# State space scan of the first block: input product made by GpSimd, decays in PSUM, sum over the states by adding DMAs

## What is computed

```
xc = silu(conv(x_proj));  dt = softplus(...);  A = -exp(A_log)
dA  = exp(dt * A[:, n])              # decay
dBx = (dt * xc) * B[:, n]            # u * B, the scan's input
h_t = dA_t * h_(t-1) + dBx_t         # along the 64 tokens of a sequence
y   = sum over n of h * C[:, n]
y   = (y + D * xc) * silu(z);  out = y @ out_proj.T
```

## Time and profile before

| | us |
|---|---|
| median of three executions | 2637.21 |
| the profiled execution | 2636.14 |
| its span | 2634.3 |

### The profile page before, as it was taken

The page is one execution under the profiler, slowest core; times in us unless marked ns, Lnnn a source line. Parts: engine busy times, 40 slices in busy tenths (PEclk is TensorE's granted clock), DMA queues, the critical chain, the costliest instruction groups (busy, mean ns, idle before and its releaser), DMA issues.

```text
span 2634.3 us, 24845 instructions
## 1 busy us (share of the span) xinstructions
PE 2179.9 (83%) x7195; PEld 1194.3 (45%) x7200; DVE 1954.9 (74%) x1963; ACT 1148.6 (44%) x2464; POOL 388.9 (15%) x310
## 2 busy tenths in 40 slices
PE   6765667988888869988898869988888869699997
PEld 2222223434554434434454434434444434588883
DVE  3699995469999986269999986269999984454543
ACT  2623330465555532265565531266565530344441
POOL 0000000001111111001111111001111111556640
PEclk9778778889999989989999989989999989799999
DMA  1210120126777761226777762226777662321210
GB/s 56 81 32 24 32 84 24 65 94 146 167 155 151 162 160 54 89 93 141 161 152 161 155 145 75 89 84 138 160 153 164 155 142 79 104 78 62 80 52 16
DMA packets 89533, 277.38 MB, mean 105 GB/s; under 512 B 10208, under 2 KB 10336, under 8 KB 87424
## 3 DMA queue, kind: packets, MB, share of 16 engines
q1 hardware_dynamic: 61056, 173.85, 21.2%
q0 software_dynamic: 28416, 102.77, 21.0%
HBM read 167.27 MB, written 4.46 MB: 65 GB/s over the span
## 4 chain that ended last, share of the span: by engine, by line
DVE 36%; PE 32%; issue 17%; ACT 10%; DMA 2%; DVEq 1%; ACTq 0%; POOL 0%; SPq 0%; POOLq 0%
DVE hs L947 13%; DVE hs L938 6%; PE acc L1218 4%; DVE hs L954 4%; PE pq L1263 3%; ACT dA L737 3%; PE acc L1342 3%; PE pq L1488 3%; PE pk L1488 2%; DMA xc<-hs 2%; DVE qp L960 2%; DVE qr L964 2%; PE pq L1271 2%; ACT qr L681 2%; ACT qr L680 2%
## 5 line engine op out<-in xcount | busy, mean ns | idle before, releaser
L947 DVE TENSOR_TENSOR_SCAN hs<-dA,hs 128x1024 f32<-128x1024 f32 x256 | 572.9, 2285 | 0.0
L737 ACT ACTIVATE dA<-dt,aneg 128x504 f32<-128x504 f32 x512 | 337.3, 709 | 511.0 <-DVE hs L947 501.8
L603 POOL DMA_DIRECT2D xc<-hs x192 | 166.3, 876 | 1443.8 <-DVE hs L954 1356.2
L1271 PE MATMUL pq<-qT,wa 128*128 128x512 f32 x768 | 347.7, 607 | 34.4 <-DVE sc L995 34.4
L1353 PE MATMUL acc<-wb,oT 128*128 128x512 f32 x768 | 365.2, 622 | 3.5 <-ACT oT L726 3.5
L938 DVE TENSOR_TENSOR hs<-u,bc 128x1024 f32<-128x1024 f32 x256 | 302.3, 1227 | 7.8 <-ACT xc L823 7.8
L954 DVE TENSOR_TENSOR hs<-hs,bc 128x1024 f32<-128x1024 f32 x256 | 305.6, 1210 | 0.0
L707 ACT ACTIVATE pr<-sc,mx 128x64 f32<-128x64 f32 x512 | 170.8, 335 | 193.1 <-DVE mx L1001 193.1
L1271 PEld LDWEIGHTS pq<-qT,wa 128*128 128x128 f32 x768 | 145.7, 194 | 213.6 <-issue 187.4
L1218 PE MATMUL acc<-xnT,wa 128*128 128x512 f32 x512 | 229.2, 601 | 11.9 <-PE acc L1218 4.4
L1353 PEld LDWEIGHTS acc<-wb,oT 128*128 128x128 f32 x768 | 146.4, 200 | 156.5 <-issue 151.8
(11 more groups left out here) (191 smaller groups left out, 3038.1 us busy)
## 6 DMA issues: line engine op xcount, KB each, us to landing
xc<-hs POOLq DMA_DIRECT2D x192, 512.0 KB, 5.7
bc<-bc_rows SPq DMA_DIRECT2D x64, 512.0 KB, 7.5
wa<-in_wq SPq DMA_DIRECT2D x64, 512.0 KB, 10.1
wb<-in_wo SPq DMA_DIRECT2D x64, 512.0 KB, 3.3
wa<-in_wx SPq DMA_DIRECT2D x16, 512.0 KB, 3.6
wa<-in_wz SPq DMA_DIRECT2D x16, 512.0 KB, 3.5
wb<-in_ow SPq DMA_DIRECT2D x16, 512.0 KB, 4.7
wk<-in_wk SPq DMA_DIRECT2D x32, 256.0 KB, 10.2
```

The costliest lines, as they stand in the source:

```text
L603: G.dma_start(xc[:, 2 * c:2 * c + 2, :], hs[:, c, :].rearrange("p (d t) -> p d t", t=T), accum_op=ALU.add).then_inc(s_y[c], 16)
L737: ins = S.activation(to[:, :, 1:SEQ], dt[:, s, :].rearrange("p (b t) -> p b t", t=SEQ)[:, :, 1:SEQ], ACT.Exp, scale=aneg[:, s, bass.ds(jj ...
L947: V.tensor_tensor_scan(out=hs[:, c, :], data0=dA[:, c % 2, :], data1=hs[:, c, :], initial=0.0, op0=ALU.mult, op1=ALU.add).then_inc(scd.sem, 1)
L1271: ins = M.matmul(pq[:, h, :], wa4(p)[:, k, h * P:(h + 1) * P], qT[:, k, :], start=(k == 0), stop=(k == KE - 1))
```

## The change

It is confined to stage 0 (`mamba and not attn`).

- GpSimd makes the scan's input u * B (`feed`), into a ring of two buffers of its own, `qp` and `qr`, which belong to the attention and are free in stage 0. Ahead of the product of chunk k it issues the adding DMA of chunk k-3 (`begin_sum`), which first waits for the product with C of k-3; the product itself waits for the scan of k-2.
- ScalarE writes the decays into PSUM (`pq` for even chunks, `pk` for odd ones). VectorE clears the first token of each sequence there, once.
- VectorE's chunk step (`scan_alone`, `state_alone`) is scan(k) from PSUM and the ring into `hs`, then the product with C of chunk k-1. A scan waits for the adding DMA of chunk k-4, which still reads the same `hs[:, c]`.
- TensorE's zero matmuls and `sum_y` are gone, and so are VectorE's additions of the banks (L1100). The sum goes into `xc` by 64 adding DMAs.

```
+        def decays(c):
+            return (pq if c % 2 == 0 else pk)[:, :, :].rearrange("p d t -> p (d t)")
+        inputs = [x[:, :, :].rearrange("p a t -> p (a t)") for x in (qp, qr)]
...
 gpsimd:
+                def begin_sum(k, at):
+                    c = k % NCH
+                    eng.wait_ge(hcd.sem, hcd.upto(0, k) + at)
+                    hold(eng)
+                    G.dma_start(xc[:, 2 * c:2 * c + 2, :], hs[:, c, :].rearrange("p (d t) -> p d t", t=T),
+                                accum_op=ALU.add).then_inc(s_y[c], 16)
+                def feed(jj, p, c, first):
+                    k, at = NCH * p + c, jj * (2 * NCH)
+                    if not first or c == 3:
+                        begin_sum(k - 3, at)
+                    if c == 0:
+                        eng.wait_ge(s_bc[p], jj * 16 + 16)
+                        hold(eng)
+                    eng.wait_ge(scd.sem, scd.upto(0, k - 2) + at)
+                    hold(eng)
+                    G.tensor_tensor(
+                        inputs[c % 2].rearrange("p (d t) -> p d t", t=T), u[:, 2 * c:2 * c + 2, :],
+                        bc[:, p, 0:1, :].to_broadcast([P, 2, T]), ALU.mult).then_inc(inr.sem, 1)
+                if mamba and not attn:
+                    eng.wait_ge(y0r.sem, y0r.upto(0, NCH - 1))
+                    for p in range(2):
+                        for c in range(NCH):
+                            feed(0, p, c, p == 0)
+                    with eng.Fori(1, NS // 2) as jj:
+                        for p in range(2):
+                            for c in range(NCH):
+                                feed(jj, p, c, False)
+                    for k in range(NS * NCH - 3, NS * NCH):
+                        begin_sum(k, 0)
+                    for c in range(NCH):
+                        eng.wait_ge(s_y[c], 16 * NS)
+                    eng.sem_inc(yad.sem, NS * NCH)
...
 scalar (decay, and ahead of the first one):
-                        to = dA[:, c % 2, d * T:(d + 1) * T].rearrange("p (b t) -> p b t", t=SEQ)
+                        to = (dA[:, c % 2, :] if attn else decays(c))[:, d * T:(d + 1) * T].rearrange(
+                            "p (b t) -> p b t", t=SEQ)
+                        if not attn and c == 0:
+                            eng.wait_ge(s_gap, 2)
...
 vector:
+                if mamba and not attn:
+                    eng.wait_ge(xnr.sem, xnr.upto(0, KE - 1))
+                    for x in (pq, pk):
+                        V.memset(x[:, :, :].rearrange("p d (b t) -> p (d b) t", t=SEQ)[:, :, 0:1], 0.0).then_inc(
+                            s_gap, 1)
...
+                def scan_alone(jj, p, c):
+                    at, k = jj * (2 * NCH), NCH * p + c
+                    if not (isinstance(jj, int) and jj == 0 and p == 0):
+                        eng.wait_ge(s_y[c], jj * 32 + 16 * p)
+                    eng.wait_ge(inr.sem, inr.upto(0, k) + at)
+                    eng.wait_ge(dar.sem, dar.upto(0, k) + at)
+                    V.tensor_tensor_scan(out=hs[:, c, :], data0=decays(c), data1=inputs[c % 2], initial=0.0,
+                                         op0=ALU.mult, op1=ALU.add).then_inc(scd.sem, 1)
+                def state_alone(jj, p, after):
+                    for c in range(NCH):
+                        scan_alone(jj, p, c)
+                        if c > 0:
+                            times_c(0, jj, p, c - 1)
+                        elif after:
+                            times_c(0, jj - 1 if p == 0 else jj, 1 - p, NCH - 1)
...
-                        for s in range(DT_TILES):
-                            V.tensor_tensor(xc[:, s, :], xc[:, s, :], y_bank(s), ALU.add).then_inc(s_ysum, 1)
...
 tensor:
-                    for s in range(DT_TILES):
-                        M.matmul(y_bank(s), zeros[:, 0:P], zeros[:, :], start=True, stop=False)
-                    def sum_y(jj, p, tail):
-                        for c in range(NCH):
-                            eng.wait_ge(hcd.sem, hcd.upto(i, NCH * p + c) + jj * (2 * NCH))
-                            for d in range(2):
-                                ins = M.matmul(y_bank(2 * c + d), ident[:, :], hs[:, c, d * T:(d + 1) * T],
-                                               start=False, stop=(tail and p == 1))
-                            ins.then_inc(yad.sem, 1)
-                    steps(eng, sum_y)
```

More of the change, by code:

```diff
@@ L194, in silu_z @@
             return sz[:, s, :] if s < 4 else xnT[:, s - 4, :]
-        def y_bank(s):
-            return acc[:, s, :] if s < TT else bank(s - TT)
+        def decays(c):
+            return (pq if c % 2 == 0 else pk)[:, :, :].rearrange("p d t -> p (d t)")
+        inputs = [x[:, :, :].rearrange("p a t -> p (a t)") for x in (qp, qr)]
         def stage(name, per):
@@ L224, in build @@
         s_aneg = sem("decay_rates_made")
-        s_ysum = sem("first_y_summed")
+        s_gap = sem("first_decays_cleared")
         ln1 = stage("ln1_variance", 1)
@@ L606, in sum_y @@
                             for d in (c - 1, c):
-                                eng.wait_ge(s_y[d], (i - 1) * (16 * NS) + jj * 32 + (16 * p + 16))
+                                eng.wait_ge(s_y[d], i * (16 * NS) + jj * 32 + (16 * p + 16))
                                 eng.sem_inc(yad.sem, 1)
+                def begin_sum(k, at):
[30 more added lines that the diff above has]
+                    eng.sem_inc(yad.sem, NS * NCH)
                 if mamba and attn:
@@ L1091, in step @@
                             rope_k(jj + 1)
-                steps(eng, step)
+                def scan_alone(jj, p, c):
[13 more added lines that the diff above has]
+                            times_c(0, jj - 1 if p == 0 else jj, 1 - p, NCH - 1)
+                if not attn:
+                    state_alone(0, 0, False)
+                    state_alone(0, 1, True)
+                    with eng.Fori(1, NS // 2) as jj:
+                        state_alone(jj, 0, True)
+                        state_alone(jj, 1, True)
+                    times_c(0, NS // 2 - 1, 1, NCH - 1)
+                else:
+                    steps(eng, step)
                 if mamba:
@@ L1096, in one @@
                     eng.wait_ge(szr.sem, szr.upto(i, DT_TILES - 1))
-                    if not attn:
-                        for s in range(DT_TILES):
-                            V.tensor_tensor(xc[:, s, :], xc[:, s, :], y_bank(s), ALU.add).then_inc(s_ysum, 1)
                     for s in range(DT_TILES):
-                        if not attn:
-                            eng.wait_ge(s_ysum, s + 1)
                         V.tensor_tensor(xc[:, s, :], xc[:, s, :], silu_z(s), ALU.mult).then_inc(yr.sem, 1)
@@ L1449, in one @@
                 if not attn:
-                    eng.wait_ge(szr.sem, szr.upto(i, DT_TILES - 1))
-                    for s in range(DT_TILES):
-                        M.matmul(y_bank(s), zeros[:, 0:P], zeros[:, :], start=True, stop=False)
-                    def sum_y(jj, p, tail):
-                        for c in range(NCH):
-                            eng.wait_ge(hcd.sem, hcd.upto(i, NCH * p + c) + jj * (2 * NCH))
-                            for d in range(2):
-                                ins = M.matmul(y_bank(2 * c + d), ident[:, :], hs[:, c, d * T:(d + 1) * T],
-                                               start=False, stop=(tail and p == 1))
-                            ins.then_inc(yad.sem, 1)
-                    steps(eng, sum_y)
                     eng.wait_ge(yr.sem, yr.upto(i, DT_TILES - 1))
```

## The result

The changed kernel took 2674.98 us (median of four; 2666.57, 2676.31, 2674.4, 2675.55) against 2635.32 (four executions of before): 1.0136 times as long, 95% interval 1.0122 to 1.0150. It is slower, and the time lies inside the range given. The profiled execution is the fastest of the four, 2666.57 us; set against the profiled one of before (2636.14) it is 30.4 us longer, where 29.8 was forecast. The medians lie 39.7 us apart, where about 30 was forecast; the traces put the difference behind stage 0, see under b1 and b2.

The account below looks back on a forecast made before the run. VectorE bounded stage 0 at 4.45 us a chunk; the moved product would make a 4.99 us chain, ending the stage 29.8 us later. 2636.14 + 29.8 = 2665.9, with the median 1.1 higher: 2667 us, range 2648 to 2702.

Parts of the forecast that it names:

- Who is held, and for how long: Stage 0: VectorE's product with C waits for GpSimd's input product, 1.2 to some 2.8 us; scans stay unstretched, 2.2 to 2.4.
- The chain of a chunk: Stage 0: semaphore to issue, DMA issue, input product and product with C sum to 4.99 us a chunk, against 4.45 before.
- The start: Beginning of stage 0: input 0 ready at about 124.6 us, scan 2 starting at 130.5.
- The end: End of stage 0: last product with C ends at 439.4 us; first product with silu(z) at 446.2, before 416.36.
- What cost nothing: Stage 0's decays, scans from PSUM, adding DMAs, loads and clearings costed at nothing; output projection starts the same, bounds 0 to 3 us.
- (1): Stage 0: the two products run beside each other, 3.4 us a chunk, 2570 us; chance 0.13, wholly or in part.
- (2): Stage 0: the scan is held too although it reads PSUM, 5.65 us a chunk, 2707 us; chance 0.05.
- (3): Stage 0: same chain with larger small terms, up to 5.4 us a chunk, 2692 us; upper part of the forecast's 0.80.

Follow-up runs that it names:

- b1: The kernel before the change run again unedited, for a second trace: 2640.94 us.
- b2: The kernel before the change run again unedited, for a third trace: 2640.82 us.
- e1: Changed kernel, with ScalarE copying row C into PSUM, where VectorE's product with C reads it: 2599.08 us.
- e3: Changed kernel, with the decays back in their two SBUF buffers, so the scan has two SBUF operands: 2696.02 us (one execution).
- e4: Changed kernel, with GpSimd multiplying u by the constant 1 instead of row B, one SBUF operand instead of two: 2610.98 us (one execution).
- e0: The changed kernel run again with no edit: 2670.56 us.
- e9: Changed kernel, with input products back on VectorE, input k+1 made right behind scan k: 2643.95 us.
- e2: Changed kernel, with GpSimd making product k before issuing the adding DMA of chunk k-3, instead of after: 2611.21 us.
- e8_c_psum_less_dma: On top of e1, TensorE sums chunk 0 of each state in two PSUM banks, a quarter fewer adding DMAs: 2595.77 us.
- e6: Changed kernel, with input products back on VectorE, each made ahead of its scan: 2647.78 us.

## Why the prediction was right, point by point

- **Who is held, and for how long.** Forecast: the product with C stretched from 1.2 to some 2.8 us, scans unstretched. Measured 2.80 and 2.28. It was read from two rows of another stage; e1, e3 and e4 show which operands it takes. The reading that a one-operand instruction on GpSimd leaves VectorE alone rested on one arrival, 1.02 us behind L560's start; those at 0.3 us are held (e4). The forecast did not hang on it.
- **The chain of a chunk.** Forecast 4.99 us, measured 4.93. By terms: semaphore to issue 0.58, measured 0.57; from the issue's start to the product's end 0.87 + 0.08 + 2.39 = 3.34, measured 3.27 (232.24 to 235.51); product with C behind it 1.07, measured 1.09. With the mean of 4.95 us, 61 chunks took 2.7 us less than forecast (301.7 against 304.4).
- **The start.** The first scan was expected at 124.6 and came at 126.81. The difference arises in the first 40 us, where the change does nothing: 32 matmuls of the first input projection took 16.83 us, 14.39 in the profiled execution of before. It is chance between executions: the changed kernel reached its first scan at 126.81 and 124.18 (e0), the kernel before at 124.43, 126.53 and 126.22 (b1, b2). TensorE's granted clock in the first 40 us is 1.00 in all five traces, so it doesn't explain the difference; the cause is open.
- **The end.** Product with C of chunk 63 forecast to end at 439.4, measured 438.86; L1173 forecast at 446.2, measured 445.72.
- **What was luck.** From first scan to L1173 I forecast 321.6 us (124.6 to 446.2) and 318.9 were measured: the stage grew by 27.0 us, not by 29.7. That the profiled executions lie 30.4 us apart, so near 29.8, needs the start that came 2.4 us later than in the profiled execution of before and 1.1 us more behind the stage, neither of which was forecast.
- **What cost nothing.** Decays: ScalarE's 675 ns into PSUM (709 into SBUF) are hidden. Scans waited 0.5 us for adding DMAs in all. TensorE's output projection starts as before. e9 confirms the sum of these for the stage.
- **Rivals.** (1), a chunk of 3.4 us, did not happen; e1 shows that it was the exclusion that stood against it. It priced that case at 2570 us; e1, without the exclusion, has 2599, so the price was 29 us too good. (2), the scan held too, is out in this kernel (2.28 us); in e3, with decays in SBUF, it is true of the first scan, and the later ones hold GpSimd instead. (3), larger small terms, was not seen in the stage; the medians lie 9 us further apart than the profiled executions, for a reason behind stage 0 that I had not listed.
- **One sentence was too sure:** "If VectorE took the lock first, ahead of the input product, the chunk would be no shorter." That holds for the order of this change. With the issue behind the product (e2) VectorE does take it first, and the chunk is 3.98 us in the mean.

## What to carry to other kernels

Before believing that work moved from VectorE to GpSimd will overlap, count the SBUF operands of the instructions that will then run beside each other. In these runs the overlap was whole when VectorE's instruction had one operand in PSUM (e1: the second operand was moved there, 71 us less than the changed kernel), and was lost with two SBUF operands on both sides. If that can't be had, order the queues so that GpSimd is the one that waits, in the shadow of an instruction that does not exclude it (e2: the same instructions, 59 us less). Blocked time is recorded as busy time, so compare an instruction's mean with what it takes elsewhere before calling an engine saturated (here 2740 ns against some 1200).

Of the kernels run here e1_c_in_psum (2599.08 us) and e8_c_psum_less_dma (2595.77 us) are the fastest, 1.5% and 1.6% below the kernel before.

## What the runs showed of the hardware

- A VectorE instruction with two SBUF operands and a GpSimd one with two exclude each other (L996 2.80 us in place of 1.20), and the one that comes second waits: VectorE in the changed kernel, GpSimd in e2. With one operand of VectorE's in PSUM they do not (1194 ns, e1; scans 2.28 us).
- A one-operand GpSimd instruction held a two-operand VectorE one only for about its first microsecond: arrivals 0.3 us behind its start took 1.25 us in place of 0.69 (stage 4 of before), one at 0.59 us took 1.88 in place of 1.20 (e4), those at 1.02 us and later took their usual time. That is for 128x1024 on GpSimd; arrivals 0.44 to 0.47 us behind a 128x512 L560 took 1.22 to 1.26 us in place of 1.21.
- A scan with two SBUF operands is held behind GpSimd's product (4.41 us, e3's first) and holds it when it comes first, letting it in, by an estimate from a product of 2.39 us, about 0.25 us before the scan's recorded end (e3).
- A scan that directly follows the input product that it depends on, and waits for by a semaphore, costs 0.12 us more a chunk than one with another instruction between them (4.57 against 4.45 us, e6 and e9). Whether the data or the semaphore makes it, no run separates.
- ScalarE writes 128 x 504 into PSUM in 675 ns, into SBUF in 709 (means; the changed kernel's stage 0, the whole of the kernel before).
